# Cross attention and a routed feed-forward layer: routing moved into the attention stage, rows stored by expert

## What is computed

```python
x = x + xattn(layernorm(x), ctx, ctx, Wq, bq, Wk, bk, Wv, bv, Wo, bo)   # 16 heads of 16, softmax inside blocks of 64
x = x + ffn(layernorm(x), gate_w, expert_bias, w_up, w_down)

def ffn(x, ...):                                  # 8 experts, 2 per token, inner width 1024
    weights = softmax(x @ gate_w.T + expert_bias)
    top_w, top_i = top_k(weights, 2);  top_w = top_w / (sum(top_w) + 1e-6)
    out = sum over e of sparse_w[e] * (gelu(x @ w_up[e].T) @ w_down[e].T)
    return layernorm(out) + x
```

## Time and profile before

| what | value |
|---|---|
| median of three timed runs | 823.88 us (823.37 to 825.12) |
| the profiled execution | 824.11 us, its span 822.2 us |
| attention | 0 to 290 us |
| routing alone | 290 to 339 us |
| expert loop | 339 to 766 us |
| last stores and combine | 766 to 822 us |
| PE busy over the span | 720.5 us (88%) |
| DVE, ACT, POOL busy | 536.4, 363.5, 441.7 us |

### The profile page before, as it was taken

One profiled execution on the slowest core, in us unless ns is written; L12 is line 12 of the kernel. 1 busy time (PEld: TensorE's weight loads), 2 busy tenths in 40 slices (PEclk: granted clock), 3 DMA queues, 4 the chain that ended last, 5 costly groups with the idle time before them and its releaser, 6 DMA issues.

```text
span 822.2 us, 20896 instructions
## 1 busy us (share of the span) xinstructions
PE 720.5 (88%) x6400; PEld 647.6 (79%) x6401; DVE 536.4 (65%) x1150; ACT 363.5 (44%) x657; POOL 441.7 (54%) x584
## 2 busy tenths in 40 slices
PE   4999999999999718599999999999999999999200
PEld 4899999999999614499899999988999999998200
DVE  4888988888888579455555555555555555555295
ACT  2877777777777403122222222222222222222284
POOL 3777877788787407424444334444443444432287
PEclk9999999999999955699999999999999999999755
DMA  4333333323342100111111111111111111110494
GB/s 157 109 105 117 110 121 99 122 99 124 99 124 89 41 7 0 52 40 53 53 51 45 45 51 45 45 51 51 51 48 42 50 45 45 51 38 27 161 314 164
DMA packets 39875, 64.54 MB, mean 78 GB/s; under 512 B 5408, under 2 KB 30240, under 8 KB 39840
## 3 DMA queue, kind: packets, MB, share of 16 engines
q1 hardware_dynamic: 31632, 42.37, 15.9%
q0 software_dynamic: 7488, 20.46, 7.7%
q10 hardware_dynamic: 720, 1.26, 0.4%
HBM read 45.46 MB, written 18.61 MB: 78 GB/s over the span
## 4 chain that ended last, share of the span: by engine, by line
PE 87%; DVE 4%; issue 3%; DMA 2%; POOL 2%; ACT 1%; SPq 0%; DVEq 0%; ACTq 0%; POOLq 0%
PE ps_a L531 25%; PE ps_b L545 25%; PE ps_b L434 7%; PE ps_a L391 4%; PE ps_b L401 4%; PE ps_c L413 4%; PE ps_c L418 3%; PE ps_a L469 3%; PE ps_a L456 2%; PE ps_c L499 2%; PE ps_c L515 2%; PE ps_a L480 1%; PE ps_c L379 1%; PE ps_a L444 1%; PE ps_c L426 1%
## 5 line engine op out<-in xcount | busy, mean ns | idle before, releaser
L531 PE MATMUL ps_a<-area,w_hi 128*128 128x256 f16 x1248 | 207.7, 274 | 1.7 <-DVE area L796 1.7
L545 PE MATMUL ps_b<-w_hi,area 128*128 x1248 | 206.4, 273 | 0.0
L1056 POOL DMA_INDIRECT y_rows<-area x78 | 77.4, 993 | 209.6 <-ACT area L941 197.7
L531 PE MATMUL ps_a<-area,w_lo 128*128 128x256 f16 x624 | 170.7, 274 | 0.0
L545 PE MATMUL ps_b<-w_lo,area 128*128 x624 | 170.1, 273 | 0.0
L936 ACT ACTIVATE area<-ps_a 128x512 f32<-128x512 f32 x156 | 93.1, 597 | 142.0 <-PE ps_a L531 142.0
L531 PEld LDWEIGHTS ps_a<-area,w_hi 128*128 x1248 | 122.5, 98 | 16.1 <-issue 2.1
L545 PEld LDWEIGHTS ps_b<-w_hi,area 128*128 128x128 f16 x1248 | 122.1, 98 | 14.1
L794 DVE TENSOR_SCALAR area<-ps_c 128x512 f16<-128x512 f32 x39 | 26.9, 691 | 151.6 <-PE ps_c L515 151.6
L806 DVE SCALAR_TENSOR_TENSOR area<-area 128x512 f16<-128x512 f32 x156 | 108.4, 695 | 5.4
L941 ACT ACTIVATE area<-ps_b 128x512 f32<-128x512 f32 x39 | 23.3, 597 | 181.1 <-PE ps_b L545 181.1
(11 more groups left out here) (129 smaller groups left out, 1253.9 us busy)
## 6 DMA issues: line engine op xcount, KB each, us to landing
area<-weights SPq DMA_DIRECT2D x32, 512.0 KB, 3.3
w_hi<-y_rows SPq DMA_DIRECT2D x32, 256.0 KB, 4.6
resid<-x_in SPq DMA_DIRECT2D x32, 128.0 KB, 2.1
area<-ctx_t SPq DMA_DIRECT2D x32, 128.0 KB, 2.1
xn_rows<-area SPq DMA_DIRECT2D x32, 128.0 KB, 1.7
out<-w_lo SPq DMA_DIRECT2D x16, 256.0 KB, 2.8
area<-xn_rows,area POOLq DMA_INDIRECT x78, 2.8
y_rows<-area POOLq DMA_INDIRECT x78
```

What stands on the lines that cost most here:

```text
L531: mm = pe.matmul(ps_h[:, q, (ic % 2) * SLOTS:(ic % 2 + 1) * SLOTS], w[:, bass.ds(first + (hc * I + ic * P), P)], r[b][:, hc, :], start=(n ...
L545: mm = pe.matmul(ps_y[:, b, v * D:(v + 1) * D], g[b][:, ic, v * P:(v + 1) * P], w[:, bass.ds(first + (EXPERT_COLS + ic * D), D)], start=(n ...
L1056: pool.indirect_dma_start(y_rows[:, :], bass.IndirectOffsetOnAxis(ap=didx[b][:, v:v + 1], axis=0), y_s[b][:, v * D:(v + 1) * D], None).the ...
```

## The change

- The loop of the attention stage is written out in full.
- Routing is cut into ten groups of tiles (4, 4, 4, 4, 4, 4, 2, 2, 2, 2). For a group whose last tile's logits come in step "seen", DVE runs `first_choice` (before q_b) and `second_choice` (after o_n) in step seen, `counts` (before q_b) and `shares` (after o_n) in step seen+1, `positions` in step seen+2. ACT takes the exponentials in seen+1, PE ranks the group with two f16 matmuls in seen+1, POOL makes two fields of the row in seen+2. Groups 8 and 9 follow behind the last step.
- A row now has 264 columns (`pay`): xn2 and 8 fields (pair number, first choice, shares, mean, variance and a scale). xn2 replaces the residual in place, and the residual is rebuilt from it in the expert loop on ACT. POOL stores each tile's rows twice (first and second choice) with indexed DMAs to `xs_rows`, at the expert's region plus the rank: one tile a step from step 9, two tiles in steps 25, 26, 29, 30, 31 and 33, and tiles 28 to 31 behind groups 8 and 9. SP fills the first 256 rows of each expert's region with blank rows in step 3.
- A table of 20 DVE operations gives each of the 39 expert tiles its expert and its first row; SP reads that row number and loads 256 rows with one plain DMA. The last tile of an expert starts so that it ends at the expert's last row; rows met twice are stored twice.
- xn moves from DVE to ACT; o_n is two operations instead of four; the two `rstd` of a step are one pair, followed by two more small POOL operations; the bias bo is a third matmul of the output projection instead of a POOL addition; the POOL addition of xn2 goes.
- In the expert loop y is scaled by the share when ACT evicts it (two activations per tile), and DVE works out destinations and shares from the loaded fields. In the combine ACT's first scaling goes, and DVE adds the two rows.

```diff
+GROUP_SIZES = (4, 4, 4, 4, 4, 4, 2, 2, 2, 2)
-        def steps(eng, lo, step):
-            for i in range(lo, FIRST):
-                step(i // 2, i % 2)
-            with eng.Fori(0, (LAST - FIRST) // 4) as n:
...
+        def group_seen(g):
+            return GROUP_AT[g + 1] - 1 + 4
+                n = min(ready - out, 1 if i < 24 else 2)      # scatter_steps: tiles stored in step i
...
@@ SP
+                if 2 * j + u == 3:
+                    for e in range(E):
+                        sp.dma_start(xs_rows[e * TOKENS:e * TOKENS + SLOTS, :]..., route_consts[:, R_BLANK:R_END])
+            sp.wait_ge(table_r, 1)
+            sp.wait_ge(pay_out, 16 * TOPK * TILES)
+                    row = sp.value_load(slot_row[0:1, bass.ds(k, 1)], ...)
+                    sp.dma_start(xg[b], xs_rows[bass.ds(row, SLOTS), :]...)
@@ PE
+                    pe.matmul(to, sel16[0:2, :], bo_rows[0:2, :], start=True, stop=False)
+                pe.matmul(ps_rank(g), tri16, m_of[size][:, :, 1:size + 1], start=True, stop=False)
+                mm = pe.matmul(ps_rank(g), ones16, c_of[size][:, :, 0:size], start=False, stop=True)
@@ DVE
-                    dve.tensor_scalar(xn, resid[...], mv1[b][:, 0:1], rs1[b], ALU.subtract, ALU.mult)
+            def second_choice(g):
+                link(dve.scalar_tensor_tensor(eq, oh[:, 0], -BIG, sh, ALU.mult, ALU.add))
+                dve.tensor_reduce(m2, over_e(eq), AX.X, ALU.max)
+                link(dve.tensor_tensor(eq, eq, per_t(g, m2), ALU.is_equal))
+                link(dve.tensor_tensor(eq, eq, per_e(g, desc_e), ALU.mult))
+                link(dve.tensor_reduce(top_i2[:, 0:size], over_e(eq), AX.X, ALU.max))
+                link(dve.tensor_tensor(oh[:, 1], per_e(g, desc_e), per_t(g, top_i2[:, 0:size]), ALU.is_equal))
+            def shares(g):
+                link(dve.tensor_reduce(top_s[:, 0:size], over_e(of(g, exx)), AX.X, ALU.add))
+                link(dve.scalar_tensor_tensor(top_den[:, 0:size], top_s[:, 0:size], GATE_EPS, e2, ALU.mult, ALU.add))
+                link(dve.tensor_scalar(top_den[:, 0:size], top_den[:, 0:size], 1.0, G_SCALE * W_SCALE, ALU.add, ALU.mult))
+                dve.reciprocal(top_rec[:, 0:size], top_den[:, 0:size])
@@ POOL
-                    pool.tensor_tensor(r, r, bo_s, ALU.add)
-                    pool.tensor_tensor(r, r, xn2, ALU.add)
+            def send(t):
+                for c in range(TOPK):
+                    pool.indirect_dma_start(xs_rows[:, :], bass.IndirectOffsetOnAxis(ap=slot_pos[:, c, t:t + 1], axis=0),
+                                            pay[:, t, :], None).then_inc(pay_out, 16)
+                for t in scatter_at.get(i, ()):           # last in POOL's step
+                    send(t)
```

More of the change, by code:

```diff
@@ L163, in program @@
[L163 to L168 removed]
+        nm1 = [carve(1) for _ in range(2)]
@@ L472, in step @@
                     rows_for_gate()
+                for g in range(NG):
+                    if in_body(g) and 2 * j + u == group_seen(g) + 1:
+                        if g == 0:
+                            pe.wait_ge(fixed_r, 5)
+                        if not valid(here(j, u, -2)[0]):
+                            pe.wait_ge(x1_r, TILES)
+                        pe.wait_ge(lg_r, min(here(j, u, -3)[0], TILES))
+                        rank(g)
                 t, half, b = here(j, u, -3)
@@ new lines, in step, with link, of @@
+                for g in range(NG):
+                    if in_body(g) and 2 * j + u == group_seen(g):
+                        second_choice(g)
+                    if in_body(g) and 2 * j + u == group_seen(g) + 1:
+                        shares(g)
+            n = [0]
+            def link(ins):
+                n[0] += 1
+                ins.then_inc(rt, 1)
+                dve.wait_ge(rt, n[0])
+            def of(g, flat, cols=E):
+                return flat[:, 0:cols * GROUP_SIZES[g]].rearrange("p (e t) -> p e t", e=cols)
@@ new lines, in _ @@
+            dve.tensor_copy(sel16[0:2, :], rc_big[0:2, R_SEL:R_SEL + P]).then_inc(bo_made, 1)
+            dve.wait_ge(bo_made, 5)
+            dve.wait_ge(fixed_r, 5)
+            steps(step)
+            for g in range(NG - 2, NG):
+                first_choice(g)
+                second_choice(g)
+                counts(g)
+                shares(g)
+                positions(g)
+            dve.wait_ge(w_lo_r, WSTEPS)
+            link(dve.tensor_tensor(over, ps_total.unsqueeze(2).to_broadcast([P, E, STEPS16]),
+                                   rcc(R_STEP, STEPS16).unsqueeze(1).to_broadcast([P, E, STEPS16]), ALU.is_gt))
@@ L882, in step @@
                     act.wait_ge(w_scaled, t + 1)
-                    act.activation(w_hi[:, bass.ds(t * WCOLS, WCOLS)], staging[b], ACT.Copy).then_inc(w_hi_r, 1)
+                    act.activation(w_hi[:, t * WCOLS:(t + 1) * WCOLS], staging[b], ACT.Copy).then_inc(w_hi_r, 1)
+                t, half, b = here(j, u, 2)
+                if valid(t):
+                    act.wait_ge(nm_r, t + 1)
+                    since(act, xt_ps, t)
+                    act.activation(xn, pay[:, t, 0:D], ACT.Identity, bias=nm1[b], scale=rs[b][:, 1:2]).then_inc(xn_r, 1)
+                for g in range(NG):
+                    if in_body(g) and 2 * j + u == group_seen(g) + 1:
+                        exps(g)
                 t, half, b = here(j, u, 0)
@@ L995, in step @@
+                for g in range(NG):
+                    if in_body(g) and i == group_seen(g) + 2:
+                        fields(g)
                 t, half, b = here(j, u, 0)
@@ L1048, in moe @@
+            done = scattered
+            for g in range(NG - 2, NG):
+                fields(g)
+                for t in range(done, GROUP_AT[g + 1]):
+                    send(t)
+                done = GROUP_AT[g + 1]
+            def moe(j, u):
                 k, half, b = here(j, u, -1)
```

646 lines of the change are left out of this document (346 added, 300 removed).

## The result

The changed kernel takes 844.11 us (842.52 to 844.76, four runs), against 824.5 us (823.37 to 825.69) for the kernel before in four runs on the same chip: ratio 1.0246, 95% interval 1.023 to 1.0262. The profiled run took 842.52 us with a span of 840.7, so 18.5 us of span have to be found.

The account below looks back on a forecast made before the run. TensorE was taken to bound attention and expert loop, with serial routing between. -25.2 + 4.0 + 12.6 + 7.0 + 5.9 - 0.4 = +3.9 on 824.11 gave 828.0 us; own range 821 to 835, over 80%: 803 to 838.

Parts of the forecast that it names:

- the serial stretch: Routing between last logits and first expert matmul: 48.8 us falls to 23.6, a gain of 25.2 us (20 to 28).
- TensorE, +4.0: Attention stage: bias matmuls +3.5 us, rank matmuls +0.8, unrolled loop -0.8, start +0.5, blank copies 0; sum +4.0.
- VectorE, 2.1 us per group, +12.6: Attention stage: added routing operations wait for POOL's w_lo and make TensorE stall, 2.1 us in each of six groups, +12.6.
- POOL's stores, +7.0: Attention steps with two tiles' stores: POOL comes late into the next step and TensorE loses time, +7.0 us (3 to 12).
- the drain, +5.9: Last attention steps: stores and positions(7) ahead of the last rstd operations in their queues add latency, +5.9 us (2 to 8).
- The combine, -0.4: Expert loop's last eviction +0.1 us, combine loses its first ACT pass, 0.5 us; POOL's addition and pow stay; -0.4.
- A: Attention stage: no port wait against w_lo, or VectorE's slack takes it; 813 to 817 us, chance 0.20.
- B: Attention stage: all added work hidden, stores included, only positions(7) in the drain; 803.6 us, chance 0.21.
- D: Expert loop: a bubble per expert tile because the 256-row load comes late; 0.5 us per tile, +20, chance 0.02.
- C: Attention stage: POOL is the bound, each store needing the 0.85 us gap, 3.6 us a tile; 841 us, chance 0.11.
- The sign that would have spoken against the forecast: Attention stage: the forecast is wrong if TensorE stays at 100% between 60 and 230 us.
- The sign of under 95% in a group's steps: Attention stage: TensorE's busy share under 95% in steps with a group, 100% in those with none.

## Why the prediction failed, step by step

The direction was right, and most mechanisms that the text named took place, but the time was not: 844.1 lies above my range. Against the profiled run (842.52, forecast 828.0) 14.5 us are missing: 8.8 in the attention stage (38.3 where I had 29.5), 4.2 from the last eviction to the end (3.8 where I had -0.4), 0.8 in the serial stretch and 0.7 in the expert loop. The steps, in its order:

- The serial stretch: 25.2 forecast, 24.4 measured. Right, with the stores as what is late there: the last starts at L+15.25 (343.76), forecast L+15.2. From there to the first expert matmul it is 9.1 us where I had 8.4; the 0.4 us for the row number in that sum was a guess, and no row isolates it.
- TensorE, +4.0: **the term that failed most**. The bias matmul was priced at a sixth of six matmuls, 0.11 us; it costs 0.41 (8.21 to 8.62 a step, both ways, by its removal), 13.1 us instead of 3.5. The row was of a stream of six alike between their own kind. A single short one between matmuls of other sizes was shown by no row, and a bound from above was missing from the range. By this price I was 9.6 us short. It is not 9.6 us of the changed kernel, though: left out of it, the matmul gives back 4.6, and the rest hides behind the other two costs. The small parts: the rank matmuls took about 0.2 a group, 1.3 us where I had 0.8; 20 steps at 0.05 are -1.0 and not the -0.8 I wrote; and the start cost nothing, blank copies included (x1 of tile 3 comes at 62.32, before at 62.06, with four bias matmuls of 0.41 in between).
- VectorE, 2.1 us per group, +12.6: the wait was where I had it (1.37 us at the head of second_choice, ended by w_lo; shares the same). Its size is 1.6 a group, so 9.4 and not 12.6; the version with w_lo held back gives 9.9 back. The path on to TensorE was only half right: I had o_t late by 0.7 and 1.4 us, and what TensorE waits for is mostly xn2, 3.1 us of 3.9 between 60 and 225. Part of what I put here was paid anyway by the matmul: each step is 0.4 us longer for VectorE too. The two terms overlap, and I added them. That this term came out 3.2 too high hid a third of the error in the one above: luck.
- POOL's stores, +7.0, and the drain, +5.9: from x1 of tile 23 to the last logits the changed kernel takes 85.5 us (243.04 to 328.51), before 63.0 (227.28 to 290.23). Of the 22.5 us more, eight bias matmuls and one group's stall are about 4.9; so the two terms together are about 17.6 where I had 12.9. With single stores the last logits come 10.4 us earlier. The queue was seen rightly; the fall of the granted clock to 0.50 behind a gap of 1.66 us was not in it. rstd(31) does stand behind four stores (4.03 us of wait); from the last x1 to the last logits it is 9.5 us, before 5.25, so 4.2 where I had 3.0.
- The combine, -0.4: +3.8. I said that POOL's addition and pow stay; I did not ask what a new form of VectorE's add does to the small addition between them. That is about 2.4 us over the groups. Another 2.5 lie behind POOL's last addition, where I had no term, and their cause is open.

Of the rivals, A (no port wait) falls with the rows of L780 and with the held-back version. B (all hidden) falls with the waits for POOL in double steps, and D with a full expert loop (140.00 of 140). C gave 841, nearest to what was measured, but by another mechanism: POOL's gap is 0.17 us before a tile's first store and 0.30 before its second, not 0.85 before both, and POOL was not the bound in single steps, since TensorE is at 36.00 of 36 in the held-back version with all stores in. The sign that would have spoken against the forecast, TensorE at 100% between 60 and 230 us, did not appear (166.12 of 170). The sign of under 95% in a group's steps came in part: 10.77 of 10.77 in the first of its three steps, 8.00 of 8.45 in the second, 7.74 of 8.23 in the third (98.49 to 134.56).

## What to carry to other kernels

A small VectorE operation of a form that waits costs what POOL has just begun, not its own 0.2 us: before new operations are placed, look at what POOL runs at that time and at which forms the rows show waiting, and let POOL's long instruction wait for the chain rather than the chain for it. Here the wait cut into pieces gained nothing, as several dependent operations followed. When TensorE sets the pace, price each added matmul from a row where one stands alone between strangers, and spread the stores on POOL's queue evenly: a burst costs its own length and then the clock.

## What the runs showed of the hardware

- Beside POOL's w_lo (2.13 us) a VectorE operation with two SBUF inputs is not done until POOL is: 0.20 us became 1.37 (L780) and, where it was still open as w_lo began, 2.68 (L788 with the stores first). Beside POOL's indexed stores L780 to L787 run free, 0.2 us each. A tensor_scalar with one input waits too, beside a POOL copy with one input: 0.90 us instead of 0.17. Free beside w_lo ran a reduction (L801, 0.21), the statistics and x1, whose one input is in PSUM (0.42 each).
- A matmul of 2 rows and 256 columns takes 0.41 us of TensorE's time out of its stream, first or last of its accumulation.
- POOL waits as well: its addition of 128x2 takes 0.44 us and not 0.19 beside VectorE's tensor_tensor add, but 0.19 beside the scalar_tensor_tensor form of the same add, which also has two SBUF inputs. Why the form decides is not shown.
- Behind 1.66 us without matmuls in 4, the granted clock was 0.50 in the next window, 0.70 in the one after.
